# Seven products with ones in front: the head of the ramp, one pair's A loads and one spill in another order

## The chip, the cores and the metric

The kernel runs on one core of a Trainium2 chip. The metric is the device time of the whole launch in microseconds (us); lower is better. TensorE (PE in the profile) multiplies, VectorE (DVE), ScalarE (ACT) and GpSimd (POOL) work beside it, and SyncE (SP) issues most of the DMAs, in the order in which its program is written.

## The reference

Everything is float32. There are 64 sequences of 32 rows by 512 features. Each sequence goes through a gated MLP with low-rank adapters that are picked by index, and then through a 32 by 32 mixing matrix that is picked by another index; both results are added to their input.

```python
def reference(x, itok_B_2_6, itok_B_0_15, W_gate, W_up, W_down, A_gate, B_gate, A_up, B_up, A_down, B_down, weights):
    def lora_add(base, inp, A, B):              # rank 16, 16 adapters, SCALE = 0.5
        Ab, Bb = A[0][itok_B_2_6], B[0][itok_B_2_6]
        t = einsum('bri,bni->bnr', Ab, inp)
        return base + einsum('bor,bnr->bno', Bb, t) * SCALE
    gate = lora_add(einsum('bnh,fh->bnf', x, W_gate), x, A_gate, B_gate)      # H = 512, F = 1376
    up = lora_add(einsum('bnh,fh->bnf', x, W_up), x, A_up, B_up)
    act = silu(gate) * up
    x = x + lora_add(einsum('bnf,hf->bnh', act, W_down), act, A_down, B_down)
    return x + einsum('bct,bcd->bdt', x, weights[itok_B_0_15])
```

## The kernel before

**Tiles and stages.** The 2,048 rows make 16 tiles of 128 rows (four sequences each), worked in eight pairs, numbered 0 to 7; `t` is the tile of a pair. The F dimension is cut into three sections (352, 512 and 512 columns), so a pair has six units (section, tile). The gate/up stage makes `act` for a pair and spills it, transposed, to DRAM (`actT_dram`); the down stage reads it back per tile (`load_actT(m, e)`), multiplies by W_down, adds the adapter and mixes.

**Split products.** Each float32 operand is split into a high part, written by ACT (`hi`, L506), and a low part, written by DVE (`lo`, L787, and L791 for the B of the adapters). A product is three matmuls: high by high, high by low, low by high (L1194 to L1196). From pair 2 (`PLAIN`) on, sections 1 and 2 of a pair use seven block products in place of eight (L1239 to L1241), which need sums of x (`sum_x`, L844 to L850) and their splits (`s_hi`, `s_lo`). The first of these pairs, pair 2, also splits several sums of weights.

**Order.** Every engine's program is written out by hand, and semaphores tie them. SP, in `pair(pr)`: load x^T of the next pair's two tiles (the second pair of loads and all later ones wait on `xT_ready` or, from pair 3's x on, on `s_ready`, since the buffer is reused), spill section 2 of the pair before, load A of the next pair's two tiles (`load_a`: eight DMAs, each with its row number read into a register, L390 and L395), and spill sections 0 and 1 of this pair. On ACT and DVE the splits of the next pair's A stand between the work of this pair: DVE runs `split_b(pr, 2, 0)`, `split_a(pr + 1, 0)`, `split_a(pr + 1, 1)`, `gating(pr, 3)`. PE starts the base products of the next pair (`base`) once `act_ready` says that the gating of unit 3 has emptied its bank.

**The ramp.** In the first microseconds PE multiplies eight blocks of ones (`ONES`, L1337), which no one reads. x of tile 0 comes in two pieces (columns 0 to 127, then 128 to 511) between the first pieces of W_gate; `base(0, 0)` waits for each piece (`x_first_ready`, `xT_ready[0]`, `w_ready`). DVE works out the adapter row numbers (`rows`, L1021 and L1025) from `which_sb` after the low part of x; POOL then gathers the first A and B rows (L447): four A, one B, four A, one B. `lora(0, 2)` needs the B of unit 2, and `base(0, 4)` the gating of units 0 and 1, which begins with `silu` (L596).

**The start of the down stage.** SP issues `load_x(0, 0)`, `load_actT(2, 0)`, `load_x(1, 1)`, then `spill(7, 2)`, which waits for the last gating, then `load_actT(3, 1)`, `store(0, 0)` and `load_x(2, 0)`. `load_actT` waits on `down_done` and `actT_ready`, `store` on `out_ready`.

## Time and profile before

| | us |
|---|---|
| median of 3 runs | 450.48 (449.51 to 450.88) |
| the profiled execution | 451.23 |
| its span, first to last instruction | 449.4 |
| PE busy | 438.8 (98% of the span) |
| DVE busy | 335.2 (75%) |
| ACT busy | 213.5 (48%) |
| POOL busy | 168.7 (38%) |

The profiled execution is a run of its own and is 0.75 us above the median. Idle time of an engine that is not the bound costs nothing. A start is exact, while the end of a matmul is modelled: two matmuls that follow each other without a pause overlap in the rows.

### The profile page before, as it was taken

To read this page: it belongs to the slowest core of one execution; us is meant where nothing else is said; L and a number is where in the kernel's file an instruction comes from. 1 tells how busy PE (TensorE), PEld (TensorE's weight loads), DVE (VectorE), ACT (ScalarE), POOL (GpSimd) and SP (SyncE) were. 2 spreads that over 40 slices of the span, in tenths; PEclk is the share of its full clock that TensorE was granted. 3 is DMA by queue.
4 is the path that set the end of the run, shared out by engine and by line. 5 is a ranking of instruction groups with operands and counts; after the bars stand their busy time and mean duration, and the time that the engine had idled before them with its cause. 6 is when DMAs were issued, how large, how long until landed. Compare 5 with 4: busy or idle time off the path is not lost.

```text
span 449.4 us, 7239 instructions
## 1 busy us (share of the span) xinstructions
PE 438.8 (98%) x2473; PEld 394.4 (88%) x2473; DVE 335.2 (75%) x622; ACT 213.5 (48%) x396; POOL 168.7 (38%) x156
## 2 busy tenths in 40 slices
PE   7999999999889999999999999999999999999997
PEld 6978888888778888888888888998999999999996
DVE  6769999888667867867867858977666776776665
ACT  6755355364444444444444445833445455444541
POOL 3712232221011211121121451675566666666620
PEclk9999999999999999999999999999999999999999
DMA  8965564446666475566565589957566666556631
GB/s 259 381 217 157 176 184 115 102 138 155 156 177 184 125 194 151 144 181 150 158 170 144 143 277 334 253 128 225 174 203 195 202 206 180 173 176 190 196 98 47
DMA packets 99699, 81.12 MB, mean 180 GB/s; under 512 B 50928, under 2 KB 83056, under 8 KB 99664
## 3 DMA queue, kind: packets, MB, share of 16 engines
q1 hardware_dynamic: 88368, 47.27, 37.7%
q0 software_dynamic: 11008, 33.30, 24.5%
q8 instruction: 19, 0.31, 0.3%
q14 instruction: 16, 0.13, 0.1%
q10 hardware_dynamic: 288, 0.10, 0.1%
HBM read 65.18 MB, written 15.47 MB: 179 GB/s over the span
## 4 chain that ended last, share of the span: by engine, by line
PE 85%; DVE 3%; DMA 3%; issue 3%; SPq 2%; POOL 2%; ACT 2%; DVEq 0%; ACTq 0%
PE bank L1363 28%; PE bank L1239 7%; PE bank L1240 7%; PE bank L1241 7%; PE bank L1194 7%; PE bank L1195 7%; PE bank L1196 7%; PE bank L1261 4%; PE bank L1262 4%; PE bank L1393 2%; POOL a_raw L447 2%; DMA b_raw<-in_b_rows,rows 2%; PE bank L1373 2%; SPq L390 1%; PE bank L1378 1%
## 5 line engine op out<-in xcount | busy, mean ns | idle before, releaser
L447 POOL DMA_INDIRECT b_raw<-in_b_rows,rows x48 | 51.5, 1073 | 194.4 <-DVE b_gu L791 192.6
L1363 PE MATMUL bank<-wd,actT_hi 128*128 128x288 f32 (+1 forms) x636 | 110.4, 295 | 1.3 <-issue 1.3
L1363 PEld LDWEIGHTS bank<-wd,actT_hi 128*128 128x128 f32 (+1 forms) x636 | 93.9, 189 | 3.0 <-issue 1.8
L447 POOL DMA_INDIRECT a_dn_raw<-in_a_dn_rows,rows x64 | 77.5, 1212 | 19.5 <-issue 19.5
L791 DVE SCALAR_TENSOR_TENSOR b_gu<-b_raw,low_rows,b_gu 128x1024 fp32r<-128x1024 f32 (+1 forms) x48 | 55.6, 1159 | 27.6 <-ACT b_gu L506 22.6
L1363 PE MATMUL bank<-wd,actT_lo 128*128 128x288 f32 (+1 forms) x318 | 68.1, 296 | 0.0
L1363 PEld LDWEIGHTS bank<-wd,actT_lo 128*128 128x128 f32 (+1 forms) x318 | 51.0, 188 | 0.0
L506 ACT ACTIVATE b_gu<-b_raw 128x1024 fp32r<-128x1024 f32 (+1 forms) x48 | 46.3, 964 | 9.9 <-DMA b_raw<-in_b_rows,rows 8.5
L596 ACT ACTIVATE act<-bank 128x512 f32<-128x512 f32 (+1 forms) x48 | 26.0, 546 | 37.3 <-PE bank L1262 37.1
L1261 PE MATMUL bank<-b_gu,tT_hi 128*128 128x512 f32 (+1 forms) x96 | 35.5, 370 | 1.4 <-DVE b_gu L791 1.4
L787 DVE TENSOR_TENSOR actT_lo<-actT_raw,actT_hi 128x1280 fp32r<-128x1280 f32 (+1 forms) x32 | 27.0, 886 | 11.6 <-issue 8.1
L898 DVE TENSOR_TENSOR act<-act,bank 128x512 f32<-128x512 f32 (+1 forms) x48 | 29.9, 622 | 7.6 <-PE bank L1262 6.2
L1262 PE MATMUL bank<-b_gu,tT_lo 128*128 128x512 f32 (+1 forms) x96 | 35.3, 368 | 0.0
L906 DVE STREAM_TRANSPOSE staging<-act 128x512 f32<-128x512 f32 (+1 forms) x48 | 31.4, 654 | 3.4
L506 ACT ACTIVATE tdT_hi<-tdT_raw 128x128 fp32r<-128x128 f32 x16 | 5.0, 311 | 59.6 <-DVE tdT_raw L1090 55.7
L1194 PE MATMUL bank<-w_gate_hi,xT_hi 128*128 128x480 f32 (+2 forms) x72 | 27.1, 376 | 2.8 <-DVE act L898 1.5
L447 POOL DMA_INDIRECT b_dn_raw<-in_b_dn_rows,rows x16 | 15.8, 990 | 34.3 <-PE bank L1363 24.2
L1195 PE MATMUL bank<-w_gate_lo,xT_hi 128*128 128x480 f32 (+2 forms) x72 | 26.7, 371 | 0.0
L1196 PE MATMUL bank<-w_gate_hi,xT_lo 128*128 128x480 f32 (+2 forms) x72 | 26.7, 371 | 0.0
L506 ACT ACTIVATE actT_hi<-actT_raw 128x1280 fp32r<-128x1280 f32 (+1 forms) x32 | 23.3, 775 | 0.0
L1261 PEld LDWEIGHTS bank<-b_gu,tT_hi 128*128 128x128 f32 x96 | 18.0, 188 | 4.8 <-DVE b_gu L791 2.1
L506 ACT ACTIVATE h_hi<-x_sb 128x224 fp32r<-128x224 f32 (+1 forms) x30 | 11.1, 414 | 22.8 <-DVE x_sb L1105 18.0
(180 smaller groups left out, 1007.9 us busy)
## 6 DMA issues: line engine op xcount, KB each, us to landing
actT_raw<-actT_dram SPq DMA_DIRECT2D x16, 640.0 KB
actT_dram<-staging SPq DMA_DIRECT2D x64, 128.0 KB
x_sb<-in_x SPq DMA_DIRECT2D x16, 256.0 KB
xT_raw<-in_xT SPq DMA_DIRECT2D x15, 256.0 KB
out<-out_sb SPq DMA_DIRECT2D x15, 256.0 KB
a_raw<-in_a_gu_rows SPq DMA_DIRECT2D x56, 64.0 KB
actT_dram<-staging SPq DMA_DIRECT2D x32, 88.0 KB
wd_raw<-in_w_down SPq DMA_DIRECT2D x10, 256.0 KB, 7.2
```

Of the source, the lines that this page charges most:

```text
L447: return pool.indirect_dma_start(dst, None, src, bass.IndirectOffsetOnAxis(ap=rows[:, tile, col:col + 1], axis=0))
L506: return nc.scalar.activation(dst, src, ACT.Copy)
L791: return nc.vector.scalar_tensor_tensor(b, raw, low_rows[:, :], b.bitcast(F32), ALU.mult, ALU.subtract)
L1194: pe.matmul(out_, x_hi, hi, start=(first and k == 0), stop=False)
L1195: pe.matmul(out_, x_hi, lo, start=False, stop=False)
L1196: last = pe.matmul(out_, x_lo, hi, start=False, stop=(stops and k == KH - 1))
L1239: pe.matmul(out_, xs[0], hi, start=(first and j == 0), stop=False, skip_group_check=True)
L1240: pe.matmul(out_, xs[0], lo, start=False, stop=False, skip_group_check=True)
L1241: last = pe.matmul(out_, xs[1], hi, start=False, stop=(j == 1), skip_group_check=True)
L1261: pe.matmul(out_, tT_hi[t][:, g, :], b, start=False, stop=False, skip_group_check=True)
L1262: pe.matmul(out_, tT_lo[t][:, g, :], b, start=False, stop=True, skip_group_check=True)\
L1363: last = pe.matmul(ps_down[e][half][:, 0:HALF], a[e][0:n, c, :], wd[0:n, c, part, at:at + HALF], start=(c == 0 and i == 0), stop=(c == NC ...
```

## The change

x of tile 0 is loaded and split in three pieces (columns 0 to 127, 128 to 255, 256 to 511). PE runs two more blocks of ones between the first and the second piece (`ONES_BETWEEN`). ACT runs one Silu of one column at its head, which puts Silu's table load there. DVE works out `rows` right after the low part of x's first piece, and POOL's gathers wait for all of x of tile 0 besides. In pair 2 alone (`pr == PLAIN`) SP loads A of pair 3 between the two loads of x^T of pair 3. In the down stage `spill(7, 2)` stands behind `load_actT(3, 1)` and `store(0, 0)`.

```diff
--- before.py
+++ after.py
@@ -40,7 +40,7 @@
 FAST = PAIRS - PLAIN
 MATRICES = ("gate", "up")
 COLS = 2 * TILE_SEQS + 3
-ONES = 8
+ONES_FIRST, ONES_BETWEEN = 8, 2
 
 PIECES = [(m, s, k) for s in range(NS) for m in ("gate", "up") for k in range(KH)]
 GU_PIECES = len(PIECES)
@@ -156,6 +156,7 @@
         which_landed = sem("which_landed")
         low_landed = sem("low_landed")
         x_first_landed = sem("x_first_landed")
+        x_second_landed = sem("x_second_landed")
         xT_landed = by_tile("xT_landed")
         a_landed = by_tile("a_landed")
         a_first_landed = by_tile("a_first_landed")
@@ -356,10 +357,13 @@
                     sp.wait_ge(rows_ready, 1)
                 if not last:
                     load_xT(pr + 1, 0)
+                    if pr == PLAIN:
+                        load_a(pr + 1, 0)
+                        load_a(pr + 1, 1)
                     load_xT(pr + 1, 1)
                 if not first:
                     spill(pr - 1, 2)
-                if not last:
+                if not last and pr != PLAIN:
                     load_a(pr + 1, 0)
                     load_a(pr + 1, 1)
                 for s in range(2):
@@ -405,8 +409,10 @@
 
             sp.dma_start(xT_raw[0][:, 0:P], xT[0:P, 0:P]).then_inc(x_first_landed, 16)
             load_gate_up(0, 1)
-            sp.dma_start(xT_raw[0][:, P:KH * P], xT[0:P, P:KH * P]).then_inc(xT_landed[0], 16)
-            load_gate_up(1, 2 * KH)
+            sp.dma_start(xT_raw[0][:, P:2 * P], xT[0:P, P:2 * P]).then_inc(x_second_landed, 16)
+            load_gate_up(1, 2)
+            sp.dma_start(xT_raw[0][:, 2 * P:KH * P], xT[0:P, 2 * P:KH * P]).then_inc(xT_landed[0], 16)
+            load_gate_up(2, 2 * KH)
             load_xT(0, 1)
             load_gate_up(2 * KH, GU_PIECES)
             pair(0, first=True)
@@ -420,9 +426,9 @@
             load_x(0, 0)
             load_actT(2, 0)
             load_x(1, 1)
-            spill(PAIRS - 1, 2)
             load_actT(3, 1)
             store(0, 0)
+            spill(PAIRS - 1, 2)
             load_x(2, 0)
             for j in range(1, TILES // 2 - 1):
                 load_actT(2 * j + 2, 0)
@@ -482,6 +488,7 @@
                 gather(mix_raw[m % 2][:, :], mix_rows, m, 2 * TILE_SEQS + 2).then_inc(mix_landed[m % 2], 16)
 
             pool.wait_ge(rows_ready, 1)
+            pool.wait_ge(xT_ready[0], 1)
             gather_first_a(0)
             gather_b(0, 0, 0)
             gather_first_a(1)
@@ -664,12 +671,17 @@
 
             sc.dma_start(which_sb[:, :, :], which).then_inc(which_landed, 16)
             sc.dma_start(low_rows[:, :], low).then_inc(low_landed, 16)
+            sc.wait_ge(ones_set, 1)
+            nc.scalar.activation(e_sb[0][:, 0:1], s_hi[0][:, 0:1].bitcast(F32), ACT.Silu)
             sc.wait_ge(x_first_landed, 16)
             hi(xT_hi[0][:, 0:P], xT_raw[0][:, 0:P]).then_inc(x_first_hi_ready, 1)
             split_weights(0, 1)
+            sc.wait_ge(x_second_landed, 16)
+            hi(xT_hi[0][:, P:2 * P], xT_raw[0][:, P:2 * P]).then_inc(x_first_hi_ready, 1)
+            split_weights(1, 2)
             sc.wait_ge(xT_landed[0], 16)
-            hi(xT_hi[0][:, P:KH * P], xT_raw[0][:, P:KH * P]).then_inc(xT_hi_ready[0], 1)
-            split_weights(1, 2 * KH)
+            hi(xT_hi[0][:, 2 * P:KH * P], xT_raw[0][:, 2 * P:KH * P]).then_inc(xT_hi_ready[0], 1)
+            split_weights(2, 2 * KH)
             split_x(0, 1)
             split_weights(2 * KH, 4 * KH)
             split_a(0, 0)
@@ -1012,9 +1024,6 @@
 
             ve.wait_ge(x_first_hi_ready, 1)
             lo(xT_lo[0][:, 0:P], xT_raw[0][:, 0:P], xT_hi[0][:, 0:P]).then_inc(x_first_ready, 1)
-            split_weights(0, 1)
-            ve.wait_ge(xT_hi_ready[0], 1)
-            lo(xT_lo[0][:, P:KH * P], xT_raw[0][:, P:KH * P], xT_hi[0][:, P:KH * P]).then_inc(xT_ready[0], 1)
 
             ve.wait_ge(which_landed, 16)
             each = [P, TILES, COLS]
@@ -1026,8 +1035,14 @@
                                     which_sb[:, TILES + 1:TILES + 2, :].to_broadcast(each), ALU.add)\
                 .then_inc(rows_ready, 1)
 
+            split_weights(0, 1)
+            ve.wait_ge(x_first_hi_ready, 2)
+            lo(xT_lo[0][:, P:2 * P], xT_raw[0][:, P:2 * P], xT_hi[0][:, P:2 * P]).then_inc(x_first_ready, 1)
+            split_weights(1, 2)
+            ve.wait_ge(xT_hi_ready[0], 1)
+            lo(xT_lo[0][:, 2 * P:KH * P], xT_raw[0][:, 2 * P:KH * P], xT_hi[0][:, 2 * P:KH * P]).then_inc(xT_ready[0], 1)
             ve.wait_ge(mask_ready, 1)
-            split_weights(1, 2 * KH)
+            split_weights(2, 2 * KH)
             split_x(0, 1)
             split_weights(2 * KH, 4 * KH)
             split_a(0, 0)
@@ -1182,13 +1197,20 @@
 
         @block.tensor
         def _(pe):
+            def ones(count):
+                for _ in range(count):
+                    pe.matmul(banks[7][:, :], s_hi[0][:, 0:P], s_hi[0][:, :], start=True, stop=True)
+
             def products(out_, s, t, m, cols, first, stops, wait=None, by_slice=False):
 
                 for k in range(KH):
+                    if by_slice and k == 1:
+                        ones(ONES_BETWEEN)
+                        pe.wait_ge(x_first_ready, 2)
+                    if by_slice and k == 2:
+                        pe.wait_ge(xT_ready[t], 1)
                     if wait is not None:
                         pe.wait_ge(w_ready, wait(k))
-                    if by_slice and k == 1:
-                        pe.wait_ge(xT_ready[t], 1)
                     x_hi, x_lo = (x_[t][:, k * P:(k + 1) * P] for x_ in (xT_hi, xT_lo))
                     hi, lo = (w_at(part, m, s, k, cols) for part in ("hi", "lo"))
                     pe.matmul(out_, x_hi, hi, start=(first and k == 0), stop=False)
@@ -1333,8 +1355,7 @@
                 lora(0, 0)
 
             pe.wait_ge(ones_set, 1)
-            for _ in range(ONES):
-                pe.matmul(banks[7][:, :], s_hi[0][:, 0:P], s_hi[0][:, :], start=True, stop=True)
+            ones(ONES_FIRST)
             base(0, 0, ramp=True, bare=True)
             base(0, 1, ramp=True, bare=True)
             base(0, 2, ramp=True)
```

ACT at the head of the program, before (`e_sb`, `s_hi` and `which_sb` are tiles in SBUF, `gu_landing` is where W_gate and W_up land):

```order
L665 DMA which_sb<-in_which 128x198
L666 DMA low_rows<-in_low 128x1
L506 ACT_TABLE_LOAD
L506 ACTIVATE xT_hi<-xT_raw 128x128
L506 ACTIVATE w_gate_hi<-gu_landing 128x352
L506 ACTIVATE xT_hi<-xT_raw 128x384
```

and after:

```order
L672 DMA which_sb<-in_which 128x198
L673 DMA low_rows<-in_low 128x1
L675 ACT_TABLE_LOAD
L675 ACTIVATE e_sbgate<-s_hi 128x1
L513 ACTIVATE xT_hi<-xT_raw 128x128
L513 ACTIVATE w_gate_hi<-gu_landing 128x352
L513 ACTIVATE xT_hi<-xT_raw 128x128
L513 ACTIVATE w_gate_hi<-gu_landing 128x352
L513 ACTIVATE xT_hi<-xT_raw 128x256
```

The head has still one table load, now that of Silu. The second one, which stood on ACT at the first Silu of pair 0, is gone. ACT there, before:

```order
L506 ACTIVATE tT_hi<-tT_raw 128x256
L506 ACTIVATE b_gu<-b_raw 128x1024
L596 ACT_TABLE_LOAD
L596 ACTIVATE act<-bank 128x352 x2
L506 ACTIVATE t_up_hi<-gu_landing 128x512 x2
```

and after:

```order
L513 ACTIVATE tT_hi<-tT_raw 128x256
L513 ACTIVATE b_gu<-b_raw 128x1024
L603 ACTIVATE act<-bank 128x352
L603 ACTIVATE act<-bank 128x352
L513 ACTIVATE t_up_hi<-gu_landing 128x512
```

One instruction has left the row between the split of B and the first Silu. SP in pair 2, before (`xT_raw` is x^T of pair 3, `staging` section 2 of pair 1, and the four last rows are one of the eight loads of A of pair 3):

```order
L328 DMA xT_raw<-in_xT 128x512 x2
L348 DMA actT_dram<-staging 32x16x64 x4
L390 TENSOR_LOAD rows
L390 ISA x2
L395 ISA
L395 DMA a_raw<-in_a_gu_rows 128x128
```

and after:

```order
L329 DMA xT_raw<-in_xT 128x512
L394 TENSOR_LOAD rows
L394 ISA x2
L399 ISA
L399 DMA a_raw<-in_a_gu_rows 128x128
...
L329 DMA xT_raw<-in_xT 128x512
L349 DMA actT_dram<-staging 32x16x64 x4
L349 DMA actT_dram<-staging 32x11x64 x4
```

All eight loads of A moved ahead of the second load of x^T and of the spill. SP at the start of the down stage, before:

```order
L400 DMA x_sb<-in_x 128x512
L348 DMA actT_dram<-staging 32x16x64 x4
L379 DMA actT_raw<-actT_dram 128x10x128
L383 DMA actT_raw<-actT_dram 96x128
L404 DMA out<-out_sb 128x512
```

and after:

```order
L404 DMA x_sb<-in_x 128x512
L383 DMA actT_raw<-actT_dram 128x10x128
L387 DMA actT_raw<-actT_dram 96x128
L408 DMA out<-out_sb 128x512
L349 DMA actT_dram<-staging 32x16x64 x4
```

The spill moved behind the load of tile 3 and the first store.

## Rows read from the trace of the kernel before

**Rows 1.** The page: busy us (share of the span) xinstructions of PE.

```profile
PE 438.8 (98%) x2473; PEld 394.4 (88%) x2473; DVE 335.2 (75%) x622; ACT 213.5 (48%) x396; POOL 168.7 (38%) x156
```

**Rows 2.** Waits of PE: us in total, times, longest us.

```profile
PE bank L1194 <- DVE act L898: 2.3, 2, 1.5
PE bank L1261 <- DVE b_gu L791: 1.4, 2, 1.2
```

**Rows 3.** Timeline of PE, pair 3: start us, us, engine, line, what [idle before].

```profile
117.30 0.45 PE L1194 MATMUL bank<-w_gate_hi,xT_hi 128*128 128x480 f32 x1 [1.46 <-DVE act L898]
...
126.75 0.43 PE L1261 MATMUL bank<-b_gu,tT_hi 128*128 128x352 f32 x1 [1.17 <-DVE b_gu L791]
```

**Rows 4.** Timeline of SP's queue, pair 2.

```profile
87.23 13.59 SPq L328 DMA_DIRECT2D xT_raw<-in_xT  x2
...
100.86 3.40 SPq L348 DMA_DIRECT2D actT_dram<-staging  x4
105.22 8.02 SPq L395 DMA_DIRECT2D a_raw<-in_a_gu_rows  x8
```

**Rows 5.** Timeline of ACT, then of DVE, around 116 us.

```profile
115.19 0.63 ACT L506 ACTIVATE w_gate_hi<-a_raw 128x512 fp32r<-128x512 f32 x1 [4.28 <-DMA a_raw<-in_a_gu_rows]
...
116.47 0.68 DVE L898 TENSOR_TENSOR act<-act,bank 128x512 f32<-128x512 f32 x1
```

**Rows 6.** Timeline of DVE, PE and DVE: what stands around the gating.

```profile
109.23 1.27 DVE L791 SCALAR_TENSOR_TENSOR b_gu<-b_raw,low_rows,b_gu 128x1024 fp32r<-128x1024 f32 x1
...
111.82 0.39 PE L1262 MATMUL bank<-b_gu,tT_lo 128*128 128x512 f32 x1
...
125.75 0.95 DVE L791 SCALAR_TENSOR_TENSOR b_gu<-b_raw,low_rows,b_gu 128x704 fp32r<-128x704 f32 x1
```

**Rows 7.** Timeline of ACT, DVE and PE around the first Silu.

```profile
30.63 1.28 ACT L596 ACT_TABLE_LOAD   x1
...
30.65 1.29 DVE L791 SCALAR_TENSOR_TENSOR b_gu<-b_raw,low_rows,b_gu 128x1024 fp32r<-128x1024 f32 x1 [0.53 <-ACT b_gu L506]
32.42 0.52 DVE L898 TENSOR_TENSOR act<-act,bank 128x352 f32<-128x352 f32 x1 [0.49 <-ACT act L596]
...
33.98 0.50 PE L1194 MATMUL bank<-t_gate_hi,xT_hi 128*128 128x512 f32 x1 [0.80 <-DVE act L898]
```

**Rows 8.** Timelines of ACT, POOL and PE in the ramp.

```profile
5.08 0.52 ACT L506 ACTIVATE xT_hi<-xT_raw 128x384 fp32r<-128x384 f32 x1 [0.68 <-DMA xT_raw<-in_xT]
...
7.10 1.11 POOL L447 DMA_INDIRECT a_raw<-in_a_gu_rows,rows  x1 [6.64 <-DVE rows L1025]
...
26.56 0.79 ACT L506 ACTIVATE b_gu<-b_raw 128x704 fp32r<-128x704 f32 x1 [1.23 <-DMA b_raw<-in_b_rows,rows]
...
26.11 0.33 PE L1194 MATMUL bank<-w_gate_hi,xT_hi 128*128 128x128 f32 x1 [0.31 <-DVE w_gate_lo L787]
...
31.99 0.50 PE L1261 MATMUL bank<-b_gu,tT_hi 128*128 128x512 f32 x1 [0.21 <-DVE b_gu L791]
```

**Rows 9.** Timeline of PE in the ramp: products of 352 columns.

```profile
9.82 0.49 PE L1196 MATMUL bank<-w_gate_hi,xT_lo 128*128 128x352 f32 x1
10.11 0.49 PE L1194 MATMUL bank<-w_up_hi,xT_hi 128*128 128x352 f32 x1
...
10.92 0.32 PE L1195 MATMUL bank<-w_up_lo,xT_hi 128*128 128x352 f32 x1
11.08 0.33 PE L1196 MATMUL bank<-w_up_hi,xT_lo 128*128 128x352 f32 x1
```

**Rows 10.** Start of the down stage: SP and PE; then windows, DMA share next to last.

```profile
300.48 0.88 SPq L379 DMA_DIRECT2D actT_raw<-actT_dram  x1
...
302.40 0.30 PE L1363 MATMUL bank<-wd,actT_hi 128*128 128x288 f32 x1
303.11 0.29 PE L1363 MATMUL bank<-wd,actT_hi 128*128 128x288 f32 x1 [0.42 <-issue]
...
302.00:303.00 1.00, 0.69 (x4) 0.50 (x3) 0.64 (x1) 0.85 (x3) 0.92 (x1) 1.00 1.00 241
```

## The prediction

> **What bounds the kernel now.** I read the page first: PE is busy for 438.8 of 449.4 us, and no other engine passes 75% [rows 1]. So the end comes earlier only by what is taken out of PE's idle time, and everything else must be followed to a pause of PE. The second view is the waits of PE: behind the ramp's first microseconds, two kinds matter, 2.3 us for a gating of DVE (longest 1.5) and 1.4 us for a split of B (longest 1.2) [rows 2]. The timeline of PE places them. The two long ones are both in pair 3, 1.46 us before 117.30 and 1.17 us before 126.75 [rows 3]; the others, 0.80, 0.21 and 0.31 us, are in the ramp between 26 and 34 us [rows 7, 8]. Third, near 302 us, PE pauses with no releaser shown [rows 10]. The idle figures are a little short, because the end of a matmul is modelled: one of 352 columns is given 0.32 us while the next starts 0.16 us after it [rows 9]. I add 0.16 to each pause.
>
> **A of pair 3 ahead of x (the main term).** The first pause waits for the gating of unit 3 of pair 2, which DVE starts at 116.47 [rows 5]. DVE runs in order, and ahead of that gating stand the low parts of A of pair 3, whose high part ACT could write only at 115.19, after 4.28 us of waiting for the DMA [rows 5]. The DMA was late because of SP's queue: SP issued the first x^T of pair 3 at 87.23, was then held by the second (both rows are one, 13.59 us long, so it issued near 100.5), spilled from 100.86 for 3.40 us, and only then issued the eight loads of A, from 105.22 for 8.02 us [rows 4]. The change puts them behind the first x^T, at about 87.6. With the first register load (about 1 us, the step from the spill's end at 104.26 to 105.22) and 8.02 us they are out near 96.6, some 4 us before SP's next command could go anyway. So the move costs the second x^T and the spill nothing, and it takes the loads out of the way of the spills behind them.
>
> What is late next? DVE has finished the B split before A at 109.23 + 1.27 = 110.50, and the gating also needs PE's product that ends at 111.82 + 0.39 = 112.21 [rows 6]. The two splits of A (0.7 us each, between these two points) fit nearly whole. So the gating starts at 112.2 in place of 116.47 and ends at 112.9. PE would be ready for it at 117.30 - 1.62 = 115.68. The first pause goes, **1.62 us**, with 2.8 us to spare.
>
> The second pause waits for a B split at 125.75 that ends at 126.70 [rows 6]; it is the end of the same DVE chain, 10.2 us behind the gating's start at 116.47. If the chain keeps its length it ends at 112.21 + 10.23 = 122.4. PE, which now has 1.62 us less behind it, would ask for it at 126.75 - 1.33 - 1.62 = 123.8. So the second pause goes too, **1.33 us**, with 1.4 us to spare. Below, the bound is that DVE's chain is stretched by something that A's lateness hid (its inputs from PE move by 1.62 and not by 4.26 us); above, I see nothing more, since no other pause of PE over 0.2 us lies between pair 3 and the down stage. Both together: 2.95 us, bounds 1.62 and 2.95.
>
> **Silu's table at the head.** The second table load takes 1.28 us at 30.63, between B's split and the first Silu [rows 7]. The head keeps one load as before, so nothing is added there but a one-column ACTIVATE; the nearest row is the 0.52 us of 384 columns [rows 8], which is its upper bound, and the head has DMA waits of ACT that hide it. Of the 1.28 us not all is on the path: DVE's first gating starts at 32.42 after 0.49 us of idle, because DVE itself is in the B split from 30.65 to 31.94 [rows 7]. So the gating, and PE's start at 33.98 that waits for it, come **0.49 us** earlier. PE's idle there, 0.80 + 0.16, is enough to take it.
>
> **x in three pieces, ones between, `rows` earlier, the gathers held.** These move the head of PE: the second K slice needs only a quarter of x, and the two ones fill its wait at 0.42 us each (512 columns at the slow rate of 0.29 for 352 [rows 9]). I cost the gain at nothing. PE pauses at 26.11 for A of tile 1 and at 31.99 for a B [rows 8], and both come from POOL's chain of ten gathers, whose last B landed for ACT at 26.56 after 1.23 us of waiting [rows 8]. Whatever PE wins before 26 us it waits away there. The cover in the other direction is about 0.5 us (0.31 + 0.16 at 26.11), and then it costs.
>
> What can move the end is the start of that chain, 7.10 now [rows 8]. It used to wait for `rows`; now it waits for x's third piece. In the trace the second piece was split on ACT at 5.08 [rows 8]; the third one is issued one DMA command later and is smaller, so it is there between 5.1 and 6.0, and with ACT (0.5), DVE (0.5), a split of W between and 0.3 to POOL's start the gathers begin at 6.5 to 7.6. The chain behind is partly bound by its own issues and partly by the DMA engines, so I take a fraction: between 0.4 us won and 0.5 us lost, **0.1 us won** as the value.
>
> **The last spill behind tile 3's load.** No engine waits for either in this trace, so the sum holds zero. But at 302.40 PE runs products of 288 columns 0.71 us apart (302.40 to 303.11), three times in a row, where 0.13 is normal (352 columns take 0.16 [rows 9]). That is 3 x 0.58 = 1.74 us lost while the DMA share is 1.00, with the load of tile 3 issued at 300.48 right behind the spill [rows 10]. The change takes the load out of this stretch and puts the spill some 5 us later. Whether the pause belongs to this traffic the profile doesn't say: bounds 0 and 1.74 us won. I take 0, because the ramp's DMAs are as dense and PE runs there unhurt, and because the spill only moves to another dense stretch.
>
> **Sum.** 1.62 + 1.33 + 0.49 + 0.10 = 3.54 us. The profiled execution took 451.23, so its like would take 447.7; it is 0.75 above the median, and against the median of 450.48 I forecast **446.9**.
>
> **The rivals.** (1) *The pause at 302 us goes as well.* For: its place and the full DMA engines. Against: no releaser is shown. 446.9 - 1.74 = 445.2. (2) *The ramp's gain on PE reaches the end.* The rate of PE in the ramp speaks for it: 352 columns are 0.29 us apart until about 10.4, the 1.2 GHz level, and 0.16 from then on, the 2.4 GHz level [rows 9], although the granted clock of the page reads full speed throughout. Before it rose PE had stood still between the first and second slice. With the pause filled by ones the rise could come before the second slice, and the ten products until 10.4 would save 0.13 each, 1.3 us: 445.6. Against it stand the pauses at 26.11 and 31.99, which wait for gathers. (The Trainium skill, "TensorE: Matmul & The Clock Gate", Part 1: The HAM clock gate, says that the slow state is the default and sustained activity releases it; by that rule the ones between do bring the rise forward, and the rows agree so far as they show it.) (3) *Only the first pause closes.* DVE's chain is held by PE's own products and ends 1.3 us later than I reckon: 446.9 + 1.3 = 448.2. (4) *The loads of A are not what holds the gating*, and both pauses return from another cause, such as DMA time for the B gathers: 446.9 + 2.95 = 449.9. The 4.28 us of ACT's wait speaks against it. (5) *Slower than before: the gathers held behind x.* If x's third piece lands behind the W pieces queued with it, POOL starts late, and each microsecond beyond 7.1 is one at 33.98. It must start after 7.1 + 0.1 + 3.5 = 10.7 to make the kernel slower at all, and at 12.5 gives 452.3. The second piece landed by 5.08, so this is remote.
>
> **How the numbers follow.** The forecast 47%, rival 1 28%, rival 2 6%, rival 3 10%, rival 4 5%, rival 5 2%, and 2% for something else near no change. Rivals 1 and 2 may fall together. The forecast's own range is 446.3 to 447.6. The range must take in rivals 1 and 3: 444.8 to 448.4. Faster means more than 0.3% (below 449.1), about what a measurement of this kernel can tell from no change: the forecast and rivals 1, 2, 3 give 0.91, rival 4 and the rest 0.07 for the same, rival 5 0.02 for slower.
>
> **What would show it.** Right: the waits of PE have no DVE act in pair 3; ACT splits A of pair 3 near 107 without waiting for a DMA; SP issues A from 88; the gating starts near 112; one table load on ACT; PE passes its `base(0, 4)` near 33.4; POOL's first gather is near 7. If the products at the slow rate end near 7 to 8 us and PE still waits near 26, my argument on the ramp holds, and if it doesn't wait there, rival 2 is right. Wrong would be a pause in pair 3 with another releaser, or a first gather past 8.

## The result: 447.67 us, and the profile after

The changed kernel takes 447.67 us (median of 6 runs, 446.79 to 448.28), the kernel before beside it 450.20 (6 runs, 449.51 to 450.88). The ratio is 0.9941, with a 95% interval from 0.9929 to 0.9954: 2.65 us less, between 2.1 and 3.2. Forecast were 446.9 and a range from 444.8 to 448.4; the forecast's own range, without the rivals, was 446.3 to 447.6, and the measured median lies just above it. The profiled execution of the changed kernel took 446.79 us, as long as its fastest run, with a span of 445.0; that of the kernel before took 451.23, longer than all six. So the two traces differ by 4.4 us where the medians differ by 2.5.

The page of the changed kernel, busy time and the granted clock in 40 slices, beside [rows 1]:

```profile
PE 438.1 (98%) x2475; PEld 393.5 (88%) x2475; DVE 335.2 (75%) x623; ACT 212.3 (48%) x397; POOL 169.7 (38%) x156
...
PEclk9999999999999999999999999999999999999999
```

PE is still the bound. Its waits in the changed kernel (us in total, times, longest), to be laid beside [rows 2]:

```profile
PE bank L1216 <- DVE w_gate_lo L799: 1.7, 2, 1.5
PE bank L1202 <- DVE s_hi L1014: 1.5, 1, 1.5
PE bank L1216 <- DVE xT_lo L799: 0.4, 1, 0.4
PE bank L1216 <- DVE act L910: 0.2, 1, 0.2
```

The 2.3 us for the gating have become 0.2, the 1.4 us for the split of B are gone, and a new wait stands first: 1.5 us for the split of an A in the ramp. The timeline of SP's queue in pair 2 of the changed kernel, beside [rows 4]:

```profile
87.52 0.36 SPq L329 DMA_DIRECT2D xT_raw<-in_xT  x1
88.62 8.00 SPq L399 DMA_DIRECT2D a_raw<-in_a_gu_rows  x8
100.75 0.34 SPq L329 DMA_DIRECT2D xT_raw<-in_xT  x1
101.14 15.31 SPq L349 DMA_DIRECT2D actT_dram<-staging  x12
```

A is issued from 88.62 instead of 105.22, and the second x^T leaves at 100.75, as before (100.5). ACT and DVE of the changed kernel around the gating of unit 3 and the next split of B, beside [rows 5, 6]:

```profile
106.80 1.15 ACT L513 ACTIVATE w_gate_hi<-a_raw 128x512 fp32r<-128x512 f32 x2
...
112.61 0.69 DVE L910 TENSOR_TENSOR act<-act,bank 128x512 f32<-128x512 f32 x1 [0.61 <-PE bank L1284]
...
122.26 0.94 DVE L803 SCALAR_TENSOR_TENSOR b_gu<-b_raw,low_rows,b_gu 128x704 fp32r<-128x704 f32 x1
```

ACT no longer waits for the DMA of A (4.28 us before), the gating starts at 112.61 instead of 116.47 and now waits for PE itself, and the split of B starts 3.5 us earlier. POOL, ACT and PE of the changed kernel in the ramp, beside [rows 7, 8]:

```profile
7.99 1.08 POOL L453 DMA_INDIRECT a_raw<-in_a_gu_rows,rows  x1 [7.54 <-DVE xT_lo L799]
...
27.39 0.79 ACT L513 ACTIVATE b_gu<-b_raw 128x704 fp32r<-128x704 f32 x1 [1.09 <-DMA b_raw<-in_b_rows,rows]
...
27.07 0.33 PE L1216 MATMUL bank<-w_gate_hi,xT_hi 128*128 128x128 f32 x1 [1.47 <-DVE w_gate_lo L799]
34.24 0.50 PE L1216 MATMUL bank<-t_gate_hi,xT_hi 128*128 128x512 f32 x1 [0.22 <-DVE act L910]
```

Here the change goes the wrong way. The gathers begin 0.89 us later (7.99 against 7.10), PE stands still for A of tile 1 for 1.47 us where it was 0.31, and it reaches `base(0, 4)` at 34.24, which is 0.26 us later than before, although the table load is gone.

### The profile page after: what moved, and what is told of

The parts are those of the page before. It is cut to its first block, busy times and chain, and to the rows that moved or that the text cites. A ratio compares the mean times of both kernels' runs of the same rounds, so it can differ in the third digit from the quotient of the medians.

```text
span 445.0 us, 7248 instructions
## 1 busy us (share of the span) xinstructions
PE 438.1 (98%) x2475; PEld 393.5 (88%) x2475; DVE 335.2 (75%) x623; ACT 212.3 (48%) x397; POOL 169.7 (38%) x156
## 4 chain that ended last, share of the span: by engine, by line
PE 92%; DMA 2%; POOL 2%; issue 2%; DVE 1%; ACT 1%; SPq 0%; POOLq 0%
PE bank L1384 28%; PE bank L1262 9%; PE bank L1263 9%; PE bank L1261 9%; PE bank L1216 7%; PE bank L1217 7%; PE bank L1218 7%; PE bank L1283 4%; PE bank L1284 4%; PE bank L1414 2%; POOL a_raw L453 2%; PE bank L1394 2%; DMA b_raw<-in_b_rows,rows 2%; DMA gu_landing<-in_w_gate 1%; PE bank L1399 1%
## 5 line engine op out<-in xcount | busy, mean ns | idle before, releaser
L1216 PE MATMUL bank<-w_up_hi,xT_hi 128*128 128x352 f32 x64 | 20.8, 324 | 0.0
```

The source lines that it names most:

```text
L1216: pe.matmul(out_, x_hi, hi, start=(first and k == 0), stop=False)
```

## How the traces are compared

There is one place from which the ramp and the rest can be told apart: PE's start of `base(0, 4)`, the first product with `t_gate_hi`. From there to one of the last products of the kernel (`last_mix_w`, 288 columns) there were, in the 14 traces of this study:

| traces | us from base(0, 4) to the end product |
|---|---|
| nine with A of pair 3 early | 407.16 to 407.31 |
| five without | 410.67 to 411.98 |

Behind the ramp, then, only the loads of A tell the kernels apart, and the nine agree within 0.15 us, wherever the last spill stands. The five spread by 1.3 us: the two pauses of pair 3 are not equally long in all of them (see e2), the first trace has the pause of [rows 10] besides, and e3 has 0.6 us at 274.8 and 0.3 us at 321 that no other trace has. All else is in the time at which PE reaches `base(0, 4)`, so the table below has, for every kernel, from its one trace, the start of the first gather, PE's wait for A of tile 1, the start of the product with that A, and `base(0, 4)`; and how many of its timed runs had a mean granted clock under 0.998. Experiments e1 to e4 ran on one chip beside 29 runs of the kernel before (450.82 us), e5 to e8 on another beside 18 (450.40), e9 to e12 on a third beside 17 (450.42); in these 64 runs of the kernel before the clock was under 0.998 in 18, 9 and 7.

| kernel | first gather | wait for A of tile 1 | A of tile 1 | base(0, 4) | clock under 0.998 | median | ratio, 95% interval |
|---|---|---|---|---|---|---|---|
| before, first trace | 7.10 | 0.31 | 26.11 | 33.98 | | 450.20 | |
| the change | 7.99 | 1.47 | 27.07 | 34.24 | 4 of 6 | 447.67 | 0.9941, 0.9929 to 0.9954 |
| e1 before again | 7.14 | 2.16 | 27.15 | 36.74 | 6 of 12 | 450.87 | 1.0005, 0.9993 to 1.0017 |
| e2 early A alone | 7.95 | none | 27.73 | 35.07 | 1 of 6 | 446.95 | 0.9916, 0.9901 to 0.9932 |
| e3 spill alone | 7.03 | 0.61 | 26.01 | 33.68 | 4 of 12 | 450.57 | 0.9993, 0.9982 to 1.0005 |
| e4 head alone | 8.00 | 2.18 | 27.74 | 37.26 | 10 of 13 | 451.80 | 1.0023, 1.0013 to 1.0033 |
| e5 Silu alone | 6.71 | 1.15 | 26.33 | 34.09 | 5 of 12 | 450.02 | 0.9986, 0.9972 to 0.9999 |
| e6 all but the head | 6.87 | 1.00 | 26.86 | 33.65 | 2 of 6 | 446.63 | 0.9923, 0.9901 to 0.9945 |
| e7 no hold | 4.60 | 0.33 | 26.80 | 33.56 | 0 of 5 | 445.59 | 0.9886, 0.9865 to 0.9908 |
| e8 no ones between | 7.88 | 1.13 | 26.57 | 34.58 | 3 of 7 | 447.23 | 0.9935, 0.9912 to 0.9958 |
| e9 ones in the pause | 8.08 | 1.23 | 27.86 | 34.61 | 0 of 6 | 447.12 | 0.9927, 0.9914 to 0.9940 |
| e10 gathers later | 10.61 | 3.31 | 29.77 | 39.24 | 12 of 12 | 451.17 | 1.0011, 0.9999 to 1.0024 |
| e11 early gathers, no ones | 4.88 | 0.20 | 26.12 | 33.21 | 0 of 5 | 445.75 | 0.9894, 0.9881 to 0.9908 |
| e12 early rows, x in two pieces | 4.61 | none | 25.90 | 33.27 | 0 of 4 | 445.24 | 0.9882, 0.9866 to 0.9897 |

What ties the first gather to A of tile 1 is the B of tile 0, which the fifth gather brings. In all 14 traces PE's product with A of tile 1 starts 6.9 to 7.2 us after ACT starts to split that B. ACT there, in the changed kernel, in e10 (gathers later) and in e7 (gathers earlier):

```profile
19.93 0.79 ACT L513 ACTIVATE b_gu<-b_raw 128x704 fp32r<-128x704 f32 x1 [1.33 <-DMA b_raw<-in_b_rows,rows]
...
22.87 0.79 ACT L513 ACTIVATE b_gu<-b_raw 128x704 fp32r<-128x704 f32 x1 [1.60 <-DMA b_raw<-in_b_rows,rows]
...
19.92 0.78 ACT L512 ACTIVATE b_gu<-b_raw 128x704 fp32r<-128x704 f32 x1
```

In the eleven traces with the first gather at 6.7 us or later ACT waits 0.9 to 1.8 us for this DMA, and in the three with the first gather before 5 us it doesn't wait, because the splits of W_up ahead of it, which wait for their own DMAs (1.18 and 0.37 us in e7), last until then. So a later start of the gathers is passed on, and an earlier one brings nothing more once that wait is closed. One trace is also a coarse measure: the kernel before and e3 have the same head, their gathers start within 0.11 us of each other in three traces, and A of tile 1 comes at 26.11, 27.15 and 26.01.

## The parts, one at a time (e1 to e6)

**e1, the kernel before, nothing changed.** It asks what of the first trace belongs to the kernel and what to that execution.

> The kernel before, once more, for its own trace and the span and clock of each run. Theory P (the pause near 302 us belongs to the DMA traffic that stands there): the pause of 1.7 us comes back in this trace, and the time is 450.2 us as before. Rival Q (it was an accident of that one execution): PE runs through that place, and the span of the profiled execution is nearer to 447.7. The mean granted clock of its runs says whether the small dips to 0.995 that the changed kernel's runs show are there before the change, too.

Measured: ratio 1.0005. Both pauses of pair 3 are there, the one near 302 us is not, and it is in none of the other 12 traces either, whether they have the new order of the spill or the old. [rows 10] showed something of that one execution; why it stood there stays open. But this trace has something else. PE of this kernel (e1) ahead of A of tile 1:

```profile
24.61 0.39 PE L1196 MATMUL bank<-b_gate_hi,xT_lo 128*128 128x512 f32 x1
27.15 0.48 PE L1194 MATMUL bank<-w_gate_hi,xT_hi 128*128 128x128 f32 x1 [2.16 <-DVE w_gate_lo L787]
27.43 0.42 PE L1195 MATMUL bank<-w_gate_lo,xT_hi 128*128 128x128 f32 x1
27.64 0.41 PE L1196 MATMUL bank<-w_gate_hi,xT_lo 128*128 128x128 f32 x1
```

and the windows of the same execution, whose third last column is the granted clock:

```profile
26.00:28.00 2.00, 0.85 (x4) 0.85 (x5) 1.36 (x3) 1.16 (x2) 0.00 (x0) 0.78 0.40 147
28.00:30.00 2.00, 2.00 (x11) 2.00 (x11) 0.60 (x1) 0.00 (x0) 0.94 (x1) 0.50 0.13 38
...
32.00:34.00 2.00, 2.00 (x6) 1.56 (x5) 1.28 (x1) 1.97 (x3) 0.00 (x0) 0.51 0.45 154
34.00:36.00 2.00, 2.00 (x11) 1.76 (x10) 1.06 (x2) 0.52 (x2) 0.94 (x1) 1.00 0.13 35
```

PE waits for 2.16 us, and then its products of 128 columns are 0.21 us apart (27.43 to 27.64) in place of 0.11: the granted clock is at its lower level, 1.2 GHz, until about 34 us. `base(0, 4)` starts at 36.74, 2.76 us later than in the first trace. So the kernel before has more than one kind of ramp, and the first trace showed the best. What the fall costs a whole run is told by the times, and this trace is of the slowest run (452.68 us, clock 0.992). Of the 76 runs of the kernel before (these 12 and the 64 beside the experiments), 36 had a mean granted clock of 0.999 or more and a median of 450.4 us, 34 had 0.995 or 0.996 and 450.8 us, and six had 0.991 or 0.992 and 452.3 us. So the usual fall goes with some 0.4 us (1.1 in the six runs of the change), and the long one of this trace, with some 2 us, is rare.

**e2, the loads of A alone.**

```diff
                     load_xT(pr + 1, 0)
+                    if pr == PLAIN:
+                        load_a(pr + 1, 0)
+                        load_a(pr + 1, 1)
                     load_xT(pr + 1, 1)
...
-                if not last:
+                if not last and pr != PLAIN:
```

> Before, with only the loads of A of pair 3 moved ahead of the second x^T. Theory: both pauses of pair 3 go, 3.0 to 3.3 us: 447.1 us on a median of 450.2. Rival (only the first pause closes): 448.6. Rival (the median's gain of 2.5 us from the whole change is all that A early gives, the rest cancels): 447.7.

Measured: 446.95, ratio 0.9916, 3.8 us less (3.1 to 4.5). This one edit gives more than the whole change. In its trace SP and DVE do what they do in the changed kernel (e2, SP's queue, then DVE):

```profile
89.45 8.00 SPq L398 DMA_DIRECT2D a_raw<-in_a_gu_rows  x8
...
113.44 0.69 DVE L901 TENSOR_TENSOR act<-act,bank 128x512 f32<-128x512 f32 x1 [0.61 <-PE bank L1265]
```

and no wait of PE stands in pair 3. What the two pauses cost, read from the distance of the starts less the usual one, was 2.99 us in the first trace and 3.28, 3.18, 4.08 and 3.25 in e1, e3, e4 and e5. Behind the pauses three more starts come late, by 0.08, 0.11 and 0.11 us in each of these traces, so that the whole is 3.3 to 4.4 us.

**e3, the spill alone.**

```diff
-            spill(PAIRS - 1, 2)
             load_actT(3, 1)
             store(0, 0)
+            spill(PAIRS - 1, 2)
```

> Before, with only the last spill moved behind tile 3's load and the first store. Theory P: the pause near 302 us goes and the time falls by 1.7 us to 448.5. Rival Q: no change, 450.2, and the trace has no such pause with the old order either.

Measured: 450.57, ratio 0.9993 (0.9982 to 1.0005): no difference that can be told.

**e4, the head alone**: x in three pieces, ones between, rows early, the gathers held; Silu, A and the spill as before. The edit is the rest of the diff shown ahead of the prediction.

> The changed kernel without the Silu at the head, without the early A and with the old place of the spill: only x in three pieces, the ones between, the earlier row numbers and the held gathers. Theory: the gathers begin 0.9 us later than before (7.99 against 7.10) and all that waits for them moves with it, so PE's start after the first Silu moves from 33.98 to 34.8 and the time rises by 0.8 us to 451.0. Rival (what PE wins at the higher rate reaches the end): 449.5 or less.

Measured: 451.80, ratio 1.0023 (1.0013 to 1.0033), 1.0 us slower. POOL and PE of this kernel (e4):

```profile
8.00 1.18 POOL L450 DMA_INDIRECT a_raw<-in_a_gu_rows,rows  x1 [7.55 <-DVE xT_lo L794]
...
27.74 0.48 PE L1211 MATMUL bank<-w_gate_hi,xT_hi 128*128 128x128 f32 x1 [2.18 <-DVE w_gate_lo L794]
```

The gathers are late, the pause is 2.18 us, and behind it the granted clock is 0.50 from 28 to 34 us. Ten of 13 runs had a mean clock under 0.998. The trace is of the slowest of them (454.25 us). But the three runs at full clock, median 451.29, are also 0.7 us above the kernel before at full clock (450.57, 11 runs on this chip), so most of the loss is there without the fall.

**e5, Silu alone.**

```diff
+            sc.wait_ge(ones_set, 1)
+            nc.scalar.activation(e_sb[0][:, 0:1], s_hi[0][:, 0:1].bitcast(F32), ACT.Silu)
             sc.wait_ge(x_first_landed, 16)
```

> The kernel before with one edit: the one-column Silu at ACT's head. What was found so far: early loads of A alone gave 446.95 against 450.82 (-3.8 us), the spill alone nothing, the head's edits alone +1.0 us. Theory H (the prediction's third term stands): one table load on ACT, the first gating of DVE 0.49 us earlier (near 31.9 in place of 32.4 in the first trace), time 0.3 to 0.6 us lower: about 450.3 on a chip where before is 450.8. Rival S (the start of PE behind the first Silu is set by B's gathers and not by the table): no difference, 450.8 within 0.2.

Measured: ratio 0.9986 (0.9972 to 0.9999), 0.6 us less, at the edge of what can be told. In the traces the gain is plain: PE's idle ahead of `base(0, 4)` for the gating is 0.78 or 0.80 us wherever the table is loaded late and this wait shows (before, e2, e3), and 0.16 to 0.23 wherever it is loaded at the head and it shows. That is about 0.57 us.

**e6, all but the head**: the edits of e2, e3 and e5 together.

> The kernel before with three of the four parts: A of pair 3 early, Silu at ACT's head, the last spill behind tile 3's load; the head of the ramp as before (x in two pieces, no ones between, rows late, gathers not held). Theory H (the head's edits cost about 1 us, the rest adds up): -3.8 for A, -0.4 for the table, 0 for the spill: 446.5 where before is 450.8, and 1.0 to 1.5 below the whole change. Rival T (the parts do not add up, and what is missing in the whole change is lost when Silu's table or the spill meet the early A): no better than the whole change, 447.7 to 448.3.

Measured: 446.63, ratio 0.9923, 3.5 us less (2.5 to 4.5). The time is what theory H said (446.5), but the kernel before took 450.40 here and not 450.8, so the gain is 3.5 us against the 4.2 of the theory. By the ratios the head costs the whole change some 0.8 us, below the 1.0 to 1.5 of the theory, and the intervals of the two ratios overlap. Nor can these runs tell that Silu still brings its 0.6 us on top of e2, whose ratio is 0.9916.

## What is wrong with the head (e7 to e12)

**e7, no hold.** Of the whole change one line is taken out.

```diff
             pool.wait_ge(rows_ready, 1)
-            pool.wait_ge(xT_ready[0], 1)
```

> The whole change without POOL's wait for all of x of tile 0: the gathers start when rows is ready. Theory H (the later start of the gathers, 7.99 in place of 7.10, makes PE's pause near 25 to 27 us longer, and with it the clock fall more often): the first gather near 5 to 6 us, PE's pause near 26 at most 0.3 us, full clock in nearly all runs, and 446.3 to 446.8 where before is 450.8. Rival C (the gathers then collide with x and the first pieces of W in the DMA queues, which is what the hold is there against): the second and third piece of x late on PE, at 447.7 or above. Rival D (the loss of the head has nothing to do with the gathers): 447.7 within 0.3.

Measured: 445.59, ratio 0.9886, 5.1 us less than before by the ratio (4.1 to 6.1), and all five runs at full clock. It is even better than theory H had it (446.3 to 446.8 where before is 450.8; it is 450.40 here). POOL and PE of this kernel (e7):

```profile
4.60 1.39 POOL L453 DMA_INDIRECT a_raw<-in_a_gu_rows,rows  x1 [4.15 <-DVE rows L1033]
...
26.80 0.33 PE L1215 MATMUL bank<-w_gate_hi,xT_hi 128*128 128x128 f32 x1 [0.33 <-DVE w_gate_lo L798]
...
33.56 0.50 PE L1215 MATMUL bank<-t_gate_hi,xT_hi 128*128 128x512 f32 x1 [0.16 <-DVE act L909]
```

The first gather is 3.4 us earlier, and the pause for A of tile 1 is 0.33 us. Most of that is not an earlier A: its product starts only 0.27 us earlier (26.80 against 27.07), since ACT no longer waits for the gather but is held by pieces of W_up (above). PE comes later. It has small waits that fit rival C, a collision with x and W (0.41 us for a piece of W_gate, 0.35 for two of W_up, 0.19 for x of tile 1), and begins tile 1 at 12.84 where the changed kernel does at 11.98; this is taken from time that it would have stood still later. The time rules rival C out, and rival D with it. The two traces show 0.68 us of the gain (`base(0, 4)` at 33.56 against 34.24), since they are of the slowest run here (446.15) and of the fastest of the change (446.79). The four runs of the change that lost clock (median 448.0) have no trace.

**e8, no ones between.**

```diff
-ONES_FIRST, ONES_BETWEEN = 8, 2
+ONES_FIRST, ONES_BETWEEN = 8, 0
```

> The whole change without the two products of ones between the first and second piece of x. Theory H: PE's early gain is waited away near 26 us in any case, so without the ones the products of the second slice run at the 1.2 GHz rate again, PE reaches A of tile 1 some 0.5 to 1 us later, waits that much less there, and the end moves by at most 0.3 us: 447.4 to 447.9 where before is 450.8. Rival E (the clock falls because PE's pause near 26 is long, and the ones make it longer): without them the pause is under 1 us, all runs have full clock, and the time is 0.5 us lower, near 447.1.

Measured: 447.23, ratio 0.9935, against 0.9941 with them: no difference. Theory H holds in the time, rival E does not (the pause is 1.13 us and three of seven runs lost clock), and theory H fails in a detail: in this trace the first slice already ran at the 2.4 GHz rate, 352 columns 0.16 us apart from 5.34 on, so the time at which the clock rises changes between executions also without the ones. PE of this kernel (e8):

```profile
5.34 0.32 PE L1217 MATMUL bank<-w_gate_lo,xT_hi 128*128 128x352 f32 x1
5.50 0.32 PE L1218 MATMUL bank<-w_gate_hi,xT_lo 128*128 128x352 f32 x1
...
26.57 0.33 PE L1216 MATMUL bank<-w_gate_hi,xT_hi 128*128 128x128 f32 x1 [1.13 <-DVE w_gate_lo L799]
...
29.31 0.63 PE L1217 MATMUL bank<-b_up_lo,xT_hi 128*128 128x512 f32 x1
29.73 0.63 PE L1218 MATMUL bank<-b_up_hi,xT_lo 128*128 128x512 f32 x1
```

And its clock fell at 28.4 (products of 512 columns are 0.43 apart from 28.88 to 31.44), where it did not fall behind a pause of 1.47 us in the changed kernel, 1.15 in e5 or 1.00 in e6. PE had worked again for 1.8 us by then, so that the pause of 1.13 us made it fall is likely and not shown.

**e9, ones in the pause.** Is it the standing still that makes the clock fall, or what else goes on there?

```diff
             def ramp_loras():
+                ones(6)
                 t_alone(1)
```

> The whole change with six more products of ones (512 columns, 0.21 us each) on PE right ahead of the small products for A of tile 1, that is, in its pause near 25 to 27 us (1.6 us in the changed kernel). Theory K (the granted clock falls to 1.2 GHz behind this pause because PE stands still in it): PE is busy there, no run shows a mean clock below 0.998, and the median is 446.7 to 447.1 where before is 450.4 to 450.8, against 447.7 for the change. Rival L (the fall comes from something else in that stretch, the DMA traffic for one): half or more of the runs stay at 0.992 to 0.996 as in the changed kernel, and the median is 447.5 to 448.

Measured: 447.12, ratio 0.9927, no run under 0.999. PE of this kernel (e9):

```profile
25.10 1.52 PE L1202 MATMUL bank<-s_hi 128*128 128x512 f32 x6
27.86 0.33 PE L1216 MATMUL bank<-w_gate_hi,xT_hi 128*128 128x128 f32 x1 [1.23 <-DVE w_gate_lo L799]
```

and its window behind the pause, the granted clock third from the end:

```profile
28.00:30.00 2.00, 2.00 (x17) 2.00 (x18) 1.46 (x4) 0.36 (x1) 0.39 (x1) 1.00 0.16 43
```

The pause had grown in this execution, since A of tile 1 came only at 27.86: without the ones PE would have stood still from about 25.3, some 2.5 us and longer than in e1. With them the clock stayed up, in all six runs, while four of six of the change, three of seven of e8 and ten of 13 of e4 lost some of it, with the gathers as late. The program of the gathers, of their DMA traffic and of the splits is unchanged, so rival L falls, and that PE stands still is the cause, as far as six runs can say. Zero of six against 17 of 26 is clear of chance, but the 26 ran on other chips; on the chip of e9 the clock was under 0.998 in all twelve runs of e10 and in seven of 17 of the kernel before, whose gathers are not held. The 0.6 us in the time is no more than its interval.

**e10, the gathers still later.**

```diff
             pool.wait_ge(rows_ready, 1)
-            pool.wait_ge(xT_ready[0], 1)
+            pool.wait_ge(w_ready, 6)
```

> The whole change with the gathers held still longer, until six pieces of W are split (the sixth ends near 9.4 us in the changed kernel, so the first gather near 9.6 in place of 7.99). Theory H (a later start of the gathers goes to the end one to one, and with it the clock): the pause before A of tile 1 is 2.5 to 3.2 us in place of 1.6, the clock falls behind it in all or nearly all runs, PE passes base(0, 4) 1.5 us later plus 1 to 2 us for the clock, and the time is 449.5 to 451 where before is 450.4 to 450.8. Rival M (the gathers are bound by the DMA traffic and not by their start): less than 0.5 us later than the change, 447.7 to 448.2.

Measured: 451.17, ratio 1.0011 (0.9999 to 1.0024): the whole gain of the change is gone, a little more than theory H had. POOL and PE of this kernel (e10):

```profile
10.61 1.08 POOL L453 DMA_INDIRECT a_raw<-in_a_gu_rows,rows  x1 [10.15 <-DVE w_up_lo L799]
...
29.77 0.48 PE L1216 MATMUL bank<-w_gate_hi,xT_hi 128*128 128x128 f32 x1 [3.31 <-DVE w_gate_lo L799]
30.04 0.41 PE L1217 MATMUL bank<-w_gate_lo,xT_hi 128*128 128x128 f32 x1
```

From the change, the first gather moved by 2.62 us (1.6 were expected), A of tile 1 by 2.70 (27.07 to 29.77), and `base(0, 4)` by 5.00. So a start of the gathers that is later than the change's does go to the end one to one, and in this trace (451.78 us, clock 0.992) the clock takes 2.3 us more on top. All twelve runs had the fall. By the times it costs less: from the change to e10 lie 3.5 us by medians and 3.1 by the ratios, 0.5 to 0.9 more than the 2.62, and the change pays for some falls itself.

**e11, early gathers without the ones between**: the edits of e7 and e8 together.

> The change without POOL's wait for x (that version gave 445.59 against 450.4) and without the two ones between the pieces of x. Theory N (PE's gain from the ones is waited away even with the early gathers, since PE still waited 0.33 us for A of tile 1 and 0.16 at base(0, 4) there): 445.4 to 445.9. Rival 2 of the prediction (with the gathers early the ones reach the end, because that wait is nearly closed): 0.7 to 1.3 us slower than with them, 446.3 to 446.9.

Measured: 445.75, ratio 0.9894, against 0.9886: the same. The ones between are worth nothing here.

**e12, early rows and x in two pieces**: e6 with one more edit, DVE works out `rows` ahead of the first split of W and of the low part of x's second piece.

```diff
             lo(xT_lo[0][:, 0:P], xT_raw[0][:, 0:P], xT_hi[0][:, 0:P]).then_inc(x_first_ready, 1)
-            split_weights(0, 1)
-            ve.wait_ge(xT_hi_ready[0], 1)
-            lo(xT_lo[0][:, P:KH * P], xT_raw[0][:, P:KH * P], xT_hi[0][:, P:KH * P]).then_inc(xT_ready[0], 1)
...
+            split_weights(0, 1)
+            ve.wait_ge(xT_hi_ready[0], 1)
+            lo(xT_lo[0][:, P:KH * P], xT_raw[0][:, P:KH * P], xT_hi[0][:, P:KH * P]).then_inc(xT_ready[0], 1)
```

> The kernel before with A of pair 3 early, Silu at ACT's head, the spill behind tile 3's load, and rows worked out ahead of the first split of W, with nothing else of the head: x in two pieces, no ones between, gathers not held. Theory P (of the head only the early rows help, by letting the gathers begin near 4.6): 445.5 to 446.0 where before is 450.4, as good as the whole change without the hold. Rival R (the third piece of x and the ones are worth something once the gathers are early): 446.3 to 446.8. Rival C (gathers ahead of x's second piece hold that piece up where it is 384 columns wide): PE waits over 0.5 us for x in the first 13 us.

Measured: 445.24, ratio 0.9882, 5.3 us less than before (4.6 to 6.0): the lowest median of all, though not to be told from e7 and e11, and with fewer edits than the change. POOL and PE of this kernel (e12):

```profile
4.61 1.35 POOL L450 DMA_INDIRECT a_raw<-in_a_gu_rows,rows  x1 [4.15 <-DVE rows L1026]
...
12.18 0.43 PE L1199 MATMUL bank<-w_gate_hi,xT_hi 128*128 128x352 f32 x1 [1.13 <-DVE xT_lo L792]
...
25.90 0.33 PE L1199 MATMUL bank<-w_gate_hi,xT_hi 128*128 128x128 f32 x1
...
33.27 0.50 PE L1199 MATMUL bank<-t_gate_hi,xT_hi 128*128 128x512 f32 x1 [0.22 <-DVE act L903]
```

Of the head only the early `rows` help, as far as these runs can tell. PE waits 1.13 us for x of tile 1 at 12.18, more than the 0.5 us of rival C though for another piece than rival C named; the clock did not fall behind it, PE then doesn't wait at all for A, and the time doesn't suffer. Between e6 and e12, which differ in nothing else, lie 1.4 us by medians and 0.38 us at `base(0, 4)`; but the trace of e6 is of its fastest run and that of e12 of its slowest, so the traces show too little. The intervals of the two ratios just miss each other (0.9897 and 0.9901).

## Why the prediction was right, and where it was not

- **Pair 3** held, step by step: no DVE act in pair 3's waits, ACT's A at 106.80 (said 107), SP from 88.62 (said 88), and the gating at 112.61 (said 112.2). The split of B ends at 123.20 (122.26 and 0.94), where I had said 122.4; that took 0.8 of the 1.4 us that I had to spare, and PE still doesn't wait. The size was 2.95 us; the two pauses cost 2.99 there and 3.2 to 4.1 in other executions, with 0.3 more for the late starts behind them, and the edit alone gave 3.8 (3.1 to 4.5). Rivals 3 and 4 fall. Going by one trace, and by the pauses alone, made this term small.
- **Silu's table**: 0.49 us put, 0.57 seen in PE's idle, 0.6 (0.04 to 1.3) alone. Right by its trace.
- **The start of the gathers is the term that failed.** I put 6.5 to 7.6 us for the first one and 0.1 us won; it was 7.99 and 0.89 later. ACT split x's third piece at 6.10, behind a piece of W that it had waited for, and DVE's low part stood from 6.67 to 7.09. From there to POOL's start passed 0.90 us where I had put 0.3, the 0.28 between 6.82 and 7.10 before. It is 0.90 in e4, e8 and e9 too, and 0.28 or 0.29 in the nine traces in which POOL waits for `rows` alone, so 0.6 of the 0.89 us go with POOL's second wait and not with x; why, no trace shows. (My own terms add up to 6.4 to 7.8 us, not 6.5 to 7.6; 7.99 is outside either.) "Past 8" was named as a sign of being wrong, and 7.99 is as good as that.
- **And its price was mis-sized**: "each microsecond is one at 33.98". It is one for the gathers' own path when they come later (e10: 2.62 us in, 2.70 out), nearly nothing in the traces when they come earlier (e7: 3.39 in, 0.27 out), and more than one where the clock falls, 2.3 us more in e10's trace and less in its median. My bound of 0.5 us lost was too small: e4 has 1.0. I had read the pause at 26.11 as a cover that makes PE's gain worthless, and did not ask what a longer one does to the clock, nor which gather holds it: it is the fifth, the B of tile 0. No row of the first trace showed a fall; e1 showed it in the kernel before.
- **The pause at 302** was costed at nothing, which is right for the median and wrong for the trace: it made the profiled execution of before some 1.7 us too long. Rival 1, to which I gave 28%, was built on a pause that none of the 13 other traces has. The times gave a hint: that execution was slower than all the runs shown.
- **Rival 2.** The rate did rise before the second slice: in the changed kernel 352 columns are 0.16 us apart from 7.14 on. PE of the changed kernel, beside [rows 9]:

```profile
7.14 0.32 PE L1217 MATMUL bank<-w_gate_lo,xT_hi 128*128 128x352 f32 x1
7.30 0.32 PE L1218 MATMUL bank<-w_gate_hi,xT_lo 128*128 128x352 f32 x1
```

  The gain was waited away at A of tile 1, as the prediction argued, and e8 and e11 confirm it. That the ones brought the rise forward isn't shown: in e8, without them, the rate was up in the first slice.
- **The spill**: nothing, as put.

So the forecast was right in its main term, and its 3.54 us against the measured 2.65 hide two errors that nearly cancel: pair 3 is worth some 0.8 more, and the head, taken for a gain of 0.1, costs about 1.0. That they cancel is luck. The rest isn't settled. The parts by their own runs, -3.8 - 0.6 + 1.0 - 0.3 = -3.7 us, are 1.0 larger than the whole; with intervals of half a microsecond or more on each this is no contradiction, and whether the parts take something from each other stays open.

## What to carry to other kernels

Take a second trace of the same kernel before its pauses are priced: here one of 1.74 us did not come back, and falls of the clock, which half of the kernel's runs have, were missing in the first. Ask also which run a trace is of: the one with the fall was the slowest of twelve, and took 2 us more for it where the usual fall costs 0.4. A pause of PE costs more than its own length where the granted clock falls behind it, so an edit that lengthens a hidden wait (here a hold on the gathers) can cost more than it moves. Where a chain of DMAs from one engine sets when a stage begins, look for what lets it start earliest: the early `rows` were the valuable part of the head, and the hold threw them away. Their worth ends where the chain behind them waits for something else.

## What the runs showed of the hardware

The granted clock fell from 2.4 to 1.2 GHz while PE stood still in the pauses of 2.16 us (e1), 2.18 (e4) and 3.31 (e10), shortly before their end, and in e8 1.8 us after the end of a pause of 1.13; it did not fall in or behind 1.47 (the change), 1.15 (e5), 1.00 (e6) or the two of 1.1 in e12. It came back while PE worked without a pause, some 3 us later in e8 (28.4 to 31.6) and 6.7 us later in e1 (27.2 to 33.9). Hence runs of one program differ in their clock. How many lose some of it depends on the gathers at the two ends: 0 of 14 runs of the kernels whose first gather starts before 5 us, and 12 of 12 where it starts at 10.6. Between them it is 17 of 26 where they are held until 8 us (the change, e4, e8) and 52 of 112 where they are not held and start at 6.7 to 7.95 in the traces (the kernel before, e2, e3, e5, e6), which is not clear of chance. The Trainium skill, "TensorE: Matmul & The Clock Gate", section "HAM oscillation — how this bites in real kernels", tells that a wait for a DMA between stretches of products sends PE back to half rate, so that the next stretch starts cold. The rows of e1, e4 and e10 agree, and e9 shows a remedy: with products of ones in the pause all six runs kept full clock.

GpSimd starts its first gather 0.28 or 0.29 us after the last thing that it waits for where it waits for `rows` alone (nine traces), and 0.90 us after it where it waits for x as well (the change, e4, e8, e9).
